# A graph network with three attention layers: GpSimd waits, at each block of eight gathers, for the landing of the block before

## The reference

```
h = x @ W                                    # 3125 x 128
e = leaky_relu(a_src[src] + a_dst[dst])      # one score for each edge and head
alpha = softmax of e over the edges of one target node
out = segment_sum(h[src] * alpha, dst)       # gather by source node, sum by target node
```

## Time and profile before

| | |
|---|---|
| timed runs | 4386.61 us median (4384.65 to 4387.99), 3 runs |
| span of the profiled execution | 5825.1 us |
| device time of that execution | not recorded apart from its span |
| GpSimd (POOL) busy | 2312.0 us, 2409 instructions |
| VectorE, TensorE, ScalarE busy | 3165.7, 3173.4, 2409.4 us |

### The profile page before, as it was taken

One profiled execution on the slowest core, in us unless ns is written; L12 is line 12 of the kernel. 1 busy time (PEld: TensorE's weight loads), 2 busy tenths in 40 slices (PEclk: granted clock), 3 DMA queues, 4 the chain that ended last, 5 costly groups with the idle time before them and its releaser, 6 DMA issues. The chain is left out here.

```text
span 5825.1 us, 61632 instructions
## 1 busy us (share of the span) xinstructions
PE 3173.4 (54%) x16208; PEld 1958.6 (34%) x16208; DVE 3165.7 (54%) x10115; ACT 2409.4 (41%) x5229; POOL 2312.0 (40%) x2409
## 2 busy tenths in 40 slices
PE   2888787623555555562155554555523555564563
PEld 1333343312333333342033333333311333343342
DVE  5999853513454554576064464555822455454466
ACT  0766630023444444443143443444433444444453
POOL 3000002074555455415545545544064545545422
PEclk7999998856777677786577777777756777777786
DMA  2111124221212222111112212211021212212110
GB/s 75 60 60 60 60 85 168 99 62 36 48 46 48 47 47 50 42 28 37 42 45 48 52 44 48 50 46 44 4 55 37 47 47 47 50 45 47 45 25 23
DMA packets 127624, 298.46 MB, mean 51 GB/s; under 512 B 45412, under 2 KB 74972, under 8 KB 123712
## 3 DMA queue, kind: packets, MB, share of 16 engines
q0 software_dynamic: 74976, 155.58, 11.6%
q1 hardware_dynamic: 52320, 139.24, 7.1%
HBM read 241.28 MB, written 53.38 MB: 51 GB/s over the span
## 5 line engine op out<-in xcount | busy, mean ns | idle before, releaser
L1400 POOL DMA_INDIRECT work<-table,lane_src x2184 | 2072.7, 949 | 1897.4 <-PE psum L1554 967.3
L1439 ACT ACTIVATE work<-work,middle_node_number 128x384 f16<-128x384 f16 x1587 | 958.0, 604 | 1997.8 <-DMA work<-table,lane_src 950.8
L1497 PE MATMUL psum<-work 128*128 128x396 bf16 (+1 forms) x5850 | 1360.1, 380 | 699.7 <-issue 464.9
L1554 PE MATMUL psum<-work 128*128 128x136 f32 x4836 | 827.7, 339 | 1004.9 <-DVE node_sums L1722 890.6
L1722 DVE TENSOR_TENSOR node_sums<-node_sums,psum 128x136 f32 x2418 | 561.3, 294 | 1455.8 <-remote 892.2
L1554 PEld LDWEIGHTS psum<-work 128*128 128x128 f32 x4836 | 778.8, 242 | 1085.0 <-issue 969.9
L1497 PEld LDWEIGHTS psum<-work 128*128 128x128 bf16 x5850 | 626.3, 109 | 1290.0 <-issue 758.1
L1442 ACT ACTIVATE work<-work 128x384 bf16<-128x384 f16 x1587 | 829.4, 523 | 50.4
L715 PE MATMUL psum<-work 128*128 128x448 f16 x2100 | 460.9, 358 | 47.4 <-issue 37.5
L744 DVE TENSOR_SCALAR work<-work 128x400 f16<-128x400 f16 x1568 | 468.3, 320 | 0.0
L772 PE MATMUL psum<-work 128*128 128x400 f16 x1568 | 342.1, 342 | 111.8 <-DVE work L744 90.9
(11 more groups left out here) (360 smaller groups left out, 2539.9 us busy)
## 6 DMA issues: line engine op xcount, KB each, us to landing
counts<-work SPq DMA_DIRECT2D x14, 2800.0 KB, 8.1
work<-counts SPq DMA_DIRECT2D x14, 2800.0 KB
work<-table,lane_src POOLq DMA_INDIRECT x2184
work<-spread SPq DMA_DIRECT2D x78, 256.0 KB
work<-masks SPq DMA_DIRECT2D x78, 128.0 KB
work<-source_rows SPq DMA_DIRECT2D x39, 192.0 KB
spread<-node_sums SPq DMA_DIRECT2D x4, 896.0 KB
table<-work SPq DMA_DIRECT2D x10, 330.0 KB
```

The source lines that it names most:

```text
L1400: pool.indirect_dma_start(m.ring[:, s % SLOTS, 0:F + H], None, m.d_table[H], bass.IndirectOffsetOnAxis(ap=m.src[:, s:s + 1], axis=0)).then ...
L1439: act.activation(away, rows_of(g, u), ACT.Abs, bias=m.low_tile[:, hi:hi + 1]).then_inc(far_known, 1)
L1497: mm = pe.matmul(aid_banks[:, k, 0:3 * (F + H)], hot_of(g, u)[:, k * P:(k + 1) * P], m.all_thirds[:, :, hi, 0:F + H], start=(hi == 0), sto ...
L1554: pe.matmul(sum_slot(s), m.onehot[b % 2][:, s % U, :], m.ring[:, s % SLOTS, :], start=True, stop=True).then_inc(product, 1)
```

## The change

Before it issues the gathers of block b, GpSimd now waits until `rows_in` of block b − 1 has reached the count that it has when all gathers of that block have landed. This holds for blocks 1 to 100 of each of the three layers.

```
             for b in range(BLOCKS):
                 if b * U >= SLOTS:
                     pool.wait_ge(product, min((b + 1) * U, REAL_STEPS) - SLOTS)
+                if b:
+                    pool.wait_ge(rows_in[(b - 1) % (SLOTS // U)], landed(b - 1))
                 for s in gathered(b):
                     pool.indirect_dma_start(m.ring[:, s % SLOTS, 0:F + H], None, m.d_table[H],
                                             bass.IndirectOffsetOnAxis(ap=m.src[:, s:s + 1], axis=0)).then_inc(rows_in[s % SLOTS // U], 16)
```

## The result

The change makes the kernel slower, and by more than was forecast: median 4953.71 us (4949.41 to 4957.97, 4 runs) against 4385.63 us (4383.68 to 4387.99, 4 runs), ratio 1.1296 (95% interval 1.128 to 1.1312), 568 us where 362 were predicted.

A forecast was written before the change was run, and what follows sets the result against it. GpSimd's gather issue was taken to bound the kernel before and after; 94 waits of 1.30 us, less 1.5 us hidden, give 120.7 us a layer, 362 in all: 4386.6 + 362 = 4748 us, range 4640 to 4840.

The forecast's parts named there:

- The timed kernel is bound by GpSimd: In the layers, a group of 64 steps takes GpSimd's gathers 72.9 us, the other engines 64.4; a layer takes 965.3 us.
- the first sum, 4395 us: Kernel before: three layers, 2896 us, plus 1499 us outside them, 8 us over the timed median.
- The crawl belongs to the recorded execution: TensorE, ScalarE and VectorE slow down during gathers only when recorded; the recording adds 1438.5 us to the timed median.
- The price of one wait, 1.30 us: At a block's first gather: 2.2 us to landing plus 0.36 to wake-up, less the 1.257 spacing; bounds 0.87 and 1.58.
- Landing to wake-up: From the end of the gathers' DMA traffic to GpSimd's wait passing: 0.36 us, bounds nothing and 0.50.
- Its sum: Per layer, 94 waits at 1.30 us put score(11) 122.2 us later; 120.7 us a layer remain, 362 us in all.
- Group 12's six waits hidden under VectorE: In each layer's last group GpSimd takes 58.1 us with the waits, just under VectorE's 59.6, so they cost nothing.
- 1.6 us, about 300 times: Sign in the profile after: GpSimd idle before each block's first gather, released by the gathers' DMA, where 0.30 stood.
- Hidden: Rival: GpSimd's gathers are ahead, so the waits cost nothing and the time stays 4387 us; chance 0.05.
- partly hidden: Rival: with gather spacing 0.949 us and 64.4 us for the others, 3.5 us a group shows, 4503 us; chance 0.03.
- Faster by relief from a crawl: Rival: pauses after each block let crawling engines work, groups falling from 73 towards 68 us, at best 4222; chance 0.04.
- Dearer: Rival: every second block's wait on a gather costs 3.3 us instead of 1.6, 255 us more, about 5000; chance 0.05.

The follow-up runs named there:

- unhindered trace: Kernel before, but from step 128 on each gather fetches rows of 32 floats from the input, on an unhindered chip: 4383.6 us, ratio 0.9997.
- the exchanged waits: Changed kernel with landing wait first, ring-slot wait second, on hindered chips: 5077.68 us (ratio 0.872) and 5388.27 us (0.9151) against the kernel before.
- the lagging wait: Changed kernel, but block b waits for the landing of block b - 2; hindered: 5831.18 us (ratio 1.0006) and 5889.77 us (1.0009) against the kernel before.
- the wait one gather on: Kernel before plus the landing wait on each block's second gather instead of its first; hindered: 5853.86 us (ratio 0.9933) and 5847.21 us (0.9939).

## Why the prediction was wrong in size and right in sign

The mechanism stood: GpSimd is the bound, each wait empties its queue, and all of the cost lies there. What failed is one term of the sum, the price of a wait.

- **The timed kernel is bound by GpSimd: right.** An unhindered trace has layers of 969.4, 982.3 and 962.8 us where 965.3 was worked out, groups of 73.4 against 72.9, and idle VectorE before each score. Outside the layers it has 1465.7 us; 1499 less the 37.8 us halt of TensorE was 1461. This choice, against the face of the profile, decided the sign. That the first sum, 4395 us, met the median within 8 us was luck in part: the halt isn't there in an unhindered execution, and it more than made up for layers that were taken 18 us too short in all.
- **The crawl belongs to the recorded execution: wrong, and without consequence.** Recorded executions on an unhindered chip don't crawl, so it isn't the recording that makes this kernel a third slower, as was said above. The trace shown of before comes from a hindered execution, its timed runs from unhindered ones.
- **The whole cost lies in the layers: right.** The layers of after last 1164.4 + 1163.8 + 1154.5 = 3482.7 us, those of the unhindered trace 2914.5: 568.2 us, the measured 568. Outside them after has 4947.6 − 3482.7 = 1464.9 us.
- **The price of one wait, 1.30 us: the step that failed.** Start to landing was right (2.2 predicted, 2.21 and 2.22 in the medians). The fit of the Trainium skill in "DMA: Bandwidth & Descriptors", Anatomy of one DMA, gives 2.16 us by estimate, close to this. That fit counts the completion in, though, and up to the semaphore the page of after has 2.5 us (part 6), somewhat more than the fit. "Landing to wake-up ... 0.36", from L886, was the time to the passing of a wait instruction (0.36 is seen again for the 255), not to the next gather. Behind such an instruction the gather starts 0.7 us later, so landing to start is 1.1 us; where the gather carries the wait itself, 0.59. Neither was in the bounds, 0 to 0.50: rows 14 was the only wait of that kind looked at, and no gather followed it. The diff of the instruction streams listed two waits on one gather from block 16 on; that they become two instructions was to be seen in no row of before.
- **Its sum.** The last gather of group 11 starts 868.5 us after the layer's first in the unhindered trace and 1061.2 in after (layer 1; 876.0 to 1055.3 and 864.3 to 1051.2 in the others): 186.3 us in the mean for 94 waits, 1.98 each, where 122.2 was predicted. (At the 94 places themselves it is 193.0 us, 2.05 each; the distances within blocks are 6.7 us a layer shorter in after than in the unhindered trace, which no run explains.) That is 64 of the 69 us a layer that are missing.
- **Group 12's six waits hidden under VectorE: wrong, by its consequence.** At 2.10 us they take group 12 from 50.3 to 62.9 us of GpSimd (63.0 in the trace of layer 1), over VectorE's 59.6, and VectorE waits 3.6, 1.9 and 3.5 us before score(12) in the three layers. Nor did group 11 cover 1.5 us: in the unhindered trace VectorE already waits 1.9, 0.9 and 1.0 us before score(11). These two make the other 5 us of a layer.
- **The tests.** "1.6 us, about 300 times": 299 gaps, of 1.85 and 2.35 us. "164 us" for the first 116 gathers: 1335.3 − 1162.3 = 173.0. "The span may even fall": it fell by 878, but mainly because only one of the two executions was hindered. The signs of being wrong that were named were a gap under 1.3 us or a difference far under 360; a dearer wait was not looked for.
- **The rivals.** Hidden and partly hidden: not so, all waits show. Faster by relief from a crawl: this is what happens on a hindered chip (0.853), but by 870 us and not through c < 1.05; on the chips of the measurement it had no place. Dearer, by gaps of 3.3 us: its time (about 5000) came nearer than the forecast, by another way: it had idle gaps of 3.3 us at every second block, and what is seen is 2.35 us at nearly every one. The 96 gaps of 3.3 us of the earlier trace rows stand in no unhindered trace.

## What to carry to other kernels

Price a wait that drains an engine's own DMAs from the start of the last one to the start of the next one behind the wait, and look whether the wait rides on that instruction or stands before it; the passing of a wait is not the start of what follows. Where span and timed runs differ by a third, ask which of the two the comparison will be made in, and build that one from rows of undisturbed stretches. A saving found on a hindered chip (15% here) may be a loss on another (13%): time the kernel before beside each variant.

## What the runs showed of the hardware

- **A gather's cost to GpSimd is nearly fixed**: 1.25 to 1.26 us apart (medians of the layers) with 128 rows of 528 or 544 bytes and with 128 rows of 128 bytes alike, 1.20 to 1.21 with 64 rows.
- **What a wait for the engine's own gathers costs depends on what is under way**: nothing for rows long landed (0.1 us for 15 waits), 0.38 us with one younger gather under way, 1.78 or 2.10 us with none.
- **Two waits on one gather are two instructions, and their order matters**: 0.59 us from landing to gather where the gather holds the wait that comes last, 1.1 where the separate one holds it, for 45 and 255 waits of after, and 0.59 in the blocks from 16 on as well once the waits are exchanged. The wait written second became the separate instruction in both orders.
- **Hindered chips.** With dense gathers (1.26 us apart) the other engines are held up and the kernel before takes 5830 to 5895 us where others give 4384. GpSimd keeps its pace. Outside the layers the hindered traces have 1501 to 1507 us against 1465 to 1467. At a spacing of 1.49 us the effect in the layers is small, at 1.81 not to be seen. It isn't tied to a chip for good: chip 8 was seen both ways. What causes it is open, as is the time that the exchanged waits, the lagging wait and the wait one gather on would take on an unhindered chip.
